# Token numbers and bias columns loaded as rows and turned by TensorE, all expert weights turned by SyncE's queue, and other orders around the expert tries

## The reference

```
x = x + attn(layernorm(x))      # linear attention, 16 heads of 32: q = k = x@Wqk + bqk, elu; v, u = silu(x@Wv + bv), silu(x@Wu + bu)
                                # kv = k^T v, out = q kv, out = layernorm(out, ln_g, ln_b); (u * out)@Wo + bo
x = x + experts(layernorm(x))   # token number picks one of 4 experts (numbers above 25000 are clipped):
                                # y = (silu(x@W[e].T) * (x@W[e].T))@W[e].T, the same ctx weights three times
x = x + ffn(layernorm(x))       # W_up, W_gate, W_down (512 x 2048), each rounded to -1, 0, 1 times its mean magnitude
```

## Time and profile before

| | |
|---|---|
| Time, median of 3 runs | 680.95 us (679.29 to 681.01) |
| The profiled execution, its own time | 680.71 us |
| its span in the profile | 678.9 us |
| TensorE busy with matmuls | 659.8 us, 97% |
| VectorE, ScalarE, GpSimd busy | 504.2, 294.8, 210.6 us |
| mean granted TensorE clock | 0.995 |

### The profile page before, as it was taken

The page is one execution under the profiler, slowest core; times in us unless marked ns, Lnnn a source line. Parts: engine busy times, 40 slices in busy tenths (PEclk is TensorE's granted clock), DMA queues, the critical chain, the costliest instruction groups (busy, mean ns, idle before and its releaser), DMA issues.

```text
span 678.9 us, 11797 instructions
## 1 busy us (share of the span) xinstructions
PE 659.8 (97%) x4435; PEld 430.0 (63%) x4465; DVE 504.2 (74%) x818; ACT 294.8 (43%) x435; POOL 210.6 (31%) x221
## 2 busy tenths in 40 slices
PE   8989999999999979999999999999999999999996
PEld 7446546546547565555556777777777777777772
DVE  6676683773754869998986986887878886676665
ACT  4475664555545254554332533342433433332331
POOL 4032543034025300001220535326343644324222
PEclk9989999999999999999999999999999999999999
DMA  7948069059058275973320111113030211101001
GB/s 197 376 150 239 1 177 258 0 126 276 31 124 261 97 269 161 252 205 94 71 55 2 30 27 28 28 28 90 1 55 2 56 62 28 28 1 63 1 1 62
DMA packets 91444, 68.15 MB, mean 100 GB/s; under 512 B 71681, under 2 KB 71681, under 8 KB 90369
## 3 DMA queue, kind: packets, MB, share of 16 engines
q1 hardware_dynamic: 88832, 59.03, 32.4%
q0 software_dynamic: 2560, 8.42, 3.4%
HBM read 42.51 MB, written 8.41 MB: 75 GB/s over the span
## 4 chain that ended last, share of the span: by engine, by line
PE 84%; DMA 7%; SPq 3%; DVE 2%; ACT 2%; issue 1%; POOL 0%; POOLq 0%; DVEq 0%; ACTq 0%
PE bank L1350 34%; PE bank L1637 28%; PE bank L1646 15%; DMA stage<-in_L_ffn_W_up_dram 4%; PE bank L1343 3%; PE bank L1516 1%; SPq L220 1%; PE bank L1538 1%; DMA late<-n 1%; PE bank L1502 1%; ACT stage L578 1%; DMA stage<-in_L_ffn_W_gate_dram 1%; DMA stage<-in_L_ffn_W_down_dram 1%; SPq L234 0%; DMA sorted_residual<-rows,pos 0%
## 5 line engine op out<-in xcount | busy, mean ns | idle before, releaser
L1637 PE MATMUL bank<-w_att,region 128*128 128x256 f16 x1024 | 127.6, 273 | 0.0
L1646 PE MATMUL bank<-region,w_moe 128*128 128x512 bf16 x482 | 113.8, 379 | 2.3 <-DVE w_moe L1260 0.8
L1637 PEld LDWEIGHTS bank<-w_att,region 128*128 128x128 bf16 x1024 | 100.1, 98 | 18.2 <-DVE tmpA L1275 0.2
L1350 PE MATMUL bank<-late,w_att 128*128 128x512 f16 x384 | 86.2, 383 | 0.3 <-DMA late<-n 0.3
L1271 DVE TENSOR_TENSOR n<-bank,n 128x512 f32<-128x512 f32 x112 | 71.4, 685 | 18.9 <-PE bank L1637 17.1
L491 POOL TENSOR_TENSOR w_moe<-tmp,w_moe 128x512 f16<-128x512 f32 x30 | 39.2, 1307 | 139.1 <-ACT w_moe L734 139.1
L1646 PEld LDWEIGHTS bank<-region,w_moe 128*128 128x128 f16 x512 | 50.0, 98 | 48.8 <-DVE w_moe L1260 1.3
L727 ACT ACTIVATE n<-n,qs 128x512 f32<-128x512 f32 x64 | 44.5, 719 | 64.6 <-DVE n L1271 64.6
L1637 PE MATMUL bank<-w_att,late 128*128 128x256 f16 x512 | 66.4, 273 | 0.0
L1350 PEld LDWEIGHTS bank<-late,w_att 128*128 128x128 f16 x384 | 37.8, 99 | 44.3 <-issue 1.8
L1637 PEld LDWEIGHTS bank<-w_att,late 128*128 128x128 bf16 x512 | 50.0, 98 | 12.1
(11 more groups left out here) (178 smaller groups left out, 1057.5 us busy)
## 6 DMA issues: line engine op xcount, KB each, us to landing
stage<-in_L_ffn_W_up_dram SPq DMA_DIRECT2D x8, 1024.0 KB, 7.2
stage<-in_L_ffn_W_gate_dram SPq DMA_DIRECT2D x8, 1024.0 KB, 6.8
rows<-sorted_residual SPq DMA_DIRECT2D x16, 257.5 KB, 3.0
stage<-in_ctx_dram SPq DMA_DIRECT2D x4, 1024.0 KB
stage<-in_L_ffn_W_down_dram SPq DMA_DIRECT2D x4, 1024.0 KB
nrm<-in_L_ffn_W_down_dram SPq DMA_DIRECT2D x4, 1024.0 KB, 7.7
rows<-in_x_dram SPq DMA_DIRECT2D x1, 3072.0 KB, 16.2
rows<-in_x_dram SPq DMA_DIRECT2D x4, 256.0 KB, 3.5
```

Source lines behind the costliest of these rows:

```text
L1350: mm = pe.matmul(dst, lhs(*step), rhs(*step), start=(start and n == 0), stop=(stop and n == len(steps) - 1))
L1637: mm = pe.matmul(wk_ps[bank][:, q * H:(q + 1) * H], w[:, c + q, k * P:(k + 1) * P], x3S_part[slot][:, h, m, k], start=(h == 0 and k == 0), ...
L1646: mm = pe.matmul(ffy_ps[t][:, :], hid[:, u, h, q, (t % 2) * P:(t % 2 + 1) * P], tern[2][:, c + q], start=(begins and q == 0 and h == 0), s ...
```

## The change

The token numbers and the four vectors are loaded as rows of 128 elements into free space of `region`, ahead of Wv. TensorE turns them into the bank `prep` between the queries' first and second parts, and VectorE copies them out to `cols` and `tokf`. Expert 0 goes the way of the others: one `ctx_half_hi`, one `ctx_half_lo`, two DMA turns. In batch 0 the load of expert 1's weights now stands ahead of `batch_turned(1)`, and ScalarE loads its Exp table before the third `magnitudes` instead of after. In the last batch the first part of `u_part(0)` stands ahead of the head products. Ahead of the tries the two first `keep_busy` have 14 and 66 matmuls instead of 52 and 16. Tiles 14 and 15 are turned by DMA as the tiles 3 to 13 are, so that their normalising and cutting fall a step or two earlier. In step 0 VectorE makes `negative(0)` after `h_mul(0)`, and `h_lo(0)` before `xs_lo(2)`; `hidden_lo` is the old `h_lo` with its wait. The diff, cut to its core:

```diff
 # SyncE: loads
-        def column_in(i, v):
-            sp.dma_start(cols[:, i], column(v), allow_slow_non_contiguous=True).then_inc(s["cols_in"], 16)
-
-        column_in(0, bqk)
+        for i, v in enumerate((bqk, bu, ln_g, ln_b)):
+            sp.dma_start(col_rows[K * i:K * i + K, :], v.rearrange("(k p) -> k p", p=P)).then_inc(s["cols_in"], 16)
+        sp.dma_start(tok[:, :], tok_v).then_inc(s["tok_in"], 16)
         sp.dma_start(att_slot[1], att_v[1]).then_inc(s["att_in1"], 16)
-        sp.dma_start(tok[:, :], tok_v, allow_slow_non_contiguous=True).then_inc(s["tok_in"], 16)
-        for i, v in ((1, bu), (2, ln_g), (3, ln_b)):
-            column_in(i, v)
...
         def weights(b):
 
-            if b > 0:
-                weights_turned(b, 0)
+            weights_turned(b, 0)
             sp.wait_ge(s["abs_done"], 3 * b + 1)
             summed_unit(b, 1)
-            if b > 0:
-                weights_turned(b, 1)
+            weights_turned(b, 1)
             sp.wait_ge(s["abs_done"], 3 * b + 2)
             summed_unit(b, 2)
-            if b > 0 and b + 1 < B:
+            if b + 1 < B:
                 expert_weights(b + 1)
-            if b + 1 < B:
                 batch_turned(b + 1)
-            if b == 0:
-                sp.wait_ge(s["ctx_mm"], 4)
-                expert_weights(1)
-            if b + 1 < B:
                 sp.wait_ge(s["abs_done"], 3 * b + 3)
                 summed_unit(b + 1, 0)
...
-        for i in range(3, NT - 2):
+        for i in range(3, NT):
             tile_turned(i)
...
 # ScalarE, batch 0
             if first:
-                ctx_hi(b, 0)
+                ctx_half_hi(b, last)
...
-                if first and m < 3:
-                    ctx_hi(b, m + 1)
...
+            act.wait_ge(s["exp_loaded"], b)
+            act.activation(spare[:, :], cols[:, 0, 0:1], ACT.Exp).then_inc(s["exp_loaded"], 1)
             if first:
                 magnitudes(b, 2)
-            act.wait_ge(s["exp_loaded"], b)
-            act.activation(spare[:, :], cols[:, 0, 0:1], ACT.Exp).then_inc(s["exp_loaded"], 1)
...
 # VectorE
+            dve.wait_ge(s["turned_rows"], 1)
+            dve.tensor_copy(cols[:].rearrange("p i k -> p (i k)"), prep[:, 0:4 * K]).then_inc(s["cols_made"], 1)
+            route(dve.tensor_copy(tokf[:, :], prep[:, 4 * K:4 * K + NT]))
...
                 routing_starts()
-                ctx_lo(b, 0)
                 routing_bases()
+                ctx_half_lo(b, last)
                 dve.wait_ge(s["x_rest"], 16)
...
                 first_stats(b + 1)
-                ctx_lo(b, 1)
                 split(3)
-                ctx_lo(b, 2)
                 first_norm(b + 1, True)
-                ctx_lo(b, 3)
...
 # VectorE, expert tries
-            if i == 0 or i + 1 in (NT - 2, NT - 1):
-                xs_lo(i + 1)
-            if i + 2 < NT - 2:
+            if i == 0:
+                xs_lo(1)
+                negative(0)
+                hidden_lo(0)
+            if i + 2 < NT:
                 xs_lo(i + 2)
-            if i + 2 in (NT - 2, NT - 1):
-                xs_norm(i + 2)
-            elif i + 3 < NT - 2:
+            if i + 3 < NT:
                 xs_norm(i + 3)
...
 # TensorE, batch 0 and the last batch
+                pe.wait_ge(s["cols_in"], 64)
+                pe.transpose(prep[:, 0:4 * K], col_rows[:, :], ident[0:4 * K, 0:4 * K])
+                pe.wait_ge(s["tok_float"], 1)
+                pe.transpose(prep[:, 4 * K:4 * K + NT], tok_rows[:, :], ident[0:NT, 0:NT]).then_inc(s["turned_rows"], 1)
                 pe.wait_ge(s["x_lo"], T)
...
             pe.wait_ge(s["w_lo"], 3)
-            if not last:
+            if last:
+                u_part(b, 0, first, [(0, 0)])
+            else:
                 for m in range(K):
                     u_part(b, m, first)
-                    if first and m < 3:
-                        ctx_part(b, m + 1)
...
-        u_part(B - 1, 0, False)
+        u_part(B - 1, 0, False, REST)
...
-        keep_busy(ps[0], 52)
+        keep_busy(ps[0], 14)
         unit_transposes(0, 0)
-        keep_busy(ps[0], 16)
+        keep_busy(ps[0], 66)
         unit_transposes(0, 1)
         keep_busy(ps[0], 16)
```

More of the change, by code:

```diff
@@ L190, in decoder @@
         ident_made pool_const started scatter_out starts_made bias_added rs1_first rs1 rs_o rs_o_last rs2 rs2_last rs3
-        w_hi_half w_hi w_lo ctx_mm ctx_hi ctx_lo ctx_half_hi ctx_half_lo ctx_in abs_done abs_mm scale_step
+        w_hi_half w_hi w_lo ctx_half_hi ctx_half_lo ctx_in abs_done abs_mm scale_step
         route_step route_pos steps_made route_mm route_read route_ready
@@ L250, in weights_turned @@
             if h:
-                sp.wait_ge(s["ctx_half_lo"], T * b)
+                sp.wait_ge(s["ctx_half_lo"], T * b + T)
             else:
-                sp.wait_ge(s["ctx_half_hi"], b)
+                sp.wait_ge(s["ctx_half_hi"], b + 1)
             sp.dma_start_transpose(out=w_moe[:, b, h].rearrange("p k (r s) -> p (k r) s", s=P),
@@ L542, in split @@
             act.activation(w_att[:, m, 0], att_slot[m], ACT.Copy).then_inc(s["w_hi"], 1)
-        def ctx_hi(b, k):
-            act.wait_ge(s["ctx_mm"], 4 * b + k + 1)
-            act.activation(w_moe[:, bass.ds(b, 1), 0, k].rearrange("p a d -> p (a d)"), prep[:, :], ACT.Copy,
-                           scale=CTX_SCALE).then_inc(s["ctx_hi"], 1)
         def ctx_half_hi(b, last):
@@ L663, in _ @@
         split(1)
-        act.wait_ge(s["cols_in"], 64)
+        act.wait_ge(s["cols_made"], 1)
         batch(0, True, False)
@@ L900, in _ @@
         first_lo(3)
+        dve.wait_ge(s["tok_in"], 16)
+        dve.tensor_copy(tok_rows[:, :], tok[:, :]).then_inc(s["tok_float"], 1)
         split(0)
         routing_members()
-        dve.wait_ge(s["cols_in"], 64)
+        dve.wait_ge(s["cols_made"], 1)
         def gated_mul(b, k, last=False):
@@ L959, in ctx_half_lo @@
         def ctx_half_lo(b, last):
-            dve.wait_ge(s["ctx_half_hi"], b)
+            dve.wait_ge(s["ctx_half_hi"], b + 1)
             hi, lo = (ctx_place(b, last, h).rearrange("p (k r s) -> p r k s", k=K, r=T) for h in range(2))
@@ L964, in ctx_half_lo @@
                                          op0=ALU.mult, op1=ALU.subtract).then_inc(s["ctx_half_lo"], 1)
-        def ctx_lo(b, k):
-            dve.wait_ge(s["ctx_hi"], 4 * b + k + 1)
-            hi = w_moe[:, bass.ds(b, 1), 0, k].rearrange("p a d -> p (a d)")
-            lo = w_moe[:, bass.ds(b, 1), 1, k].rearrange("p a d -> p (a d)")
-            dve.scalar_tensor_tensor(out=lo, in0=prep[:, :], scalar=CTX_SCALE, in1=hi, op0=ALU.mult,
-                                     op1=ALU.subtract).then_inc(s["ctx_lo"], 1)
         def q_elu(b, m, bank=None):
@@ L1196, in weight_sum, with hidden_lo @@
             dve.tensor_tensor(dst[j], a[j], b[j], op).then_inc(s[done], 1)
+        def hidden_lo(i):
+            dve.wait_ge(s["h_hi"], i + 1)
+            dve.tensor_tensor(hT[:, 1], th_ps[:, :], hT[:, 0], ALU.subtract).then_inc(s["h_lo"], 1)
         def expert_step(i):
@@ L1223, in expert_step @@
                 negative(i)
-            dve.wait_ge(s["h_hi"], i + 1)
-            dve.tensor_tensor(hT[:, 1], th_ps[:, :], hT[:, 0], ALU.subtract).then_inc(s["h_lo"], 1)
+            if i > 0:
+                hidden_lo(i)
             if i in (9, 10):
@@ L1239, in _ @@
         xs_norm(2)
-        negative(0)
         for i in range(STEPS):
@@ L1353, in _ @@
         ones_b = ones[:, :].bitcast(BF16)
+        REST = [(1, 0), (0, 1)]
         def keep_busy(bank, n):
@@ L1408, in project, with u_part @@
                 product(*operands(t)).then_inc(s["wo_mm"], 1)
-        def u_part(b, m, first):
+        def u_part(b, m, first, pairs=PARTS):
+            operands = (acc[m % 2][:, :], lambda i, j, k: w_att[:, 2, j, k, m * P:(m + 1) * P], lambda i, j, k: xT[:, i, k])
+            if pairs == REST:
+                partial(*operands, pairs, range(K), False, True).then_inc(s["u_mm"], 1)
+                return
             if m < 2:
@@ L1417, in u_part @@
                 pe.wait_ge(s["u_act"], K * b + m - 1)
-            product(acc[m % 2][:, :], lambda i, j, k: w_att[:, 2, j, k, m * P:(m + 1) * P],
-                    lambda i, j, k: xT[:, i, k]).then_inc(s["u_mm"], 1)
+            mm = partial(*operands, pairs, range(K), True, pairs == PARTS)
+            if pairs == PARTS:
+                mm.then_inc(s["u_mm"], 1)
         def batch(b, first, last):
@@ L1482, in batch @@
                 transposes(tr[t % 2], lambda k: qT[:, k, t * P:(t + 1) * P]).then_inc(s["tk_mm"], 1)
-            if first:
-                pe.wait_ge(s["stage_in0"], 16)
-                ctx_part(b, 0)
             pe.wait_ge(s["w_lo"], 3)
-            if not last:
+            if last:
+                u_part(b, 0, first, [(0, 0)])
+            else:
                 for m in range(K):
                     u_part(b, m, first)
-                    if first and m < 3:
-                        ctx_part(b, m + 1)
```

35 lines of the change are left out of this document (13 added, 22 removed).

## The result

The changed kernel is slower: 684.8 us (median of 8 runs, 683.4 to 686.1) against 680.45 us before (8 runs), ratio 1.0060, 95% interval 1.0048 to 1.0071. Forecast was 678.5. The profiled execution took 683.6 us with a span of 681.9, against 680.7 and 678.9.

What follows compares the result with a forecast made beforehand. TensorE, busy 97% of the span, was taken as the bound. Gains of 0.6 + 0.7 + 0.2 + 0.9 = 2.4 us took the profiled 680.7 to 678.3, 678.5 as a median; range 676.6 to 680.8.

Steps and rivals of the forecast that it cites:

- tiles 14 and 15: Late steps of the tries: turning these by DMA saves TensorE two turns of 0.44 us each, 0.9 us in all.
- The clock: Rival: granted clock falls in a new wait, costing 1.7 us once (680.2), both places 681.9; chance 0.2.
- the first of its two places: Batch 0, between `kv_mm` and `o_mm`: TensorE would stand still for 3 us, from 51 to 54.
- The second place: Ahead of the tries, behind 14 constant matmuls: a new TensorE wait of 2.5 us, from 234.6 to 237.1.
- The front: Batch 0's loads and ScalarE's chain up to batch 1's first query: gain 0.3 to 1.3 us, taken as 0.6.
- Last batch: Ahead of `kv_mm`: four matmuls of `u_part(0)` fill TensorE's 0.73 us wait for ScalarE's copies; gain 0.7 us.
- Entry and step 0: Passage into the tries: `h_mul(0)` right after silu gains 1.1 us, delay ahead loses 0.9; net gain 0.2.
- the 66 matmuls: Constant matmuls before the second turn of signs: 3.9 us instead of 0.95, turn 1.36 late, 0.48 covered; loss 0.9.

Runs made afterwards that it cites:

- with GpSimd after `weight_sum`: Changed kernel with GpSimd's `x3_lo(0)` made to wait until VectorE's `weight_sum` of step 12 is over; ratio 1.0048 to the kernel before.
- filling the wait: Changed kernel with 90 constant matmuls put on TensorE between `kv_mm` and `o_mm` of batch 0; ratio 1.0027 to the kernel before.
- The rows alone: Kernel before with only token numbers and bias columns loaded as rows and turned by TensorE; ratio 0.9992 to the kernel before.

## Why the prediction was wrong

**The step that failed: tiles 14 and 15.** I took 0.44 us twice off TensorE, "with TensorE back to back before and behind". That is true of the turn. It left out that the same edit gives VectorE another `xs_lo` ahead of step 12, turns the operand of `xs_lo` from a bank into SBUF, and makes `weight_sum` start behind GpSimd, which holds it for 4.46 us instead of 1.22 and TensorE with it, for 0.41 and 2.21 us. Forecast −0.9; measured +2.7 in the tail and +3.1 in the median. The row that warned stood in the trace of before, an `xs_norm` of 2.39 us beside GpSimd where others take 0.54, and I did not read it, since nothing waited for it.

The Trainium skill (SBUF — State Buffer, SBUF: two separate sides) says that VectorE and GpSimd share a pair of ports under an exclusive lock, and that whichever starts first holds it "for the whole instruction". It names VectorE's instructions in a two-port fast mode, and those with two SBUF inputs beside a GpSimd instruction that reads SBUF. Two traces here agree: `weight_sum` of 1.22 us took 4.46 behind GpSimd, `xs_lo(15)` 3.76 instead of 0.68 (with GpSimd after `weight_sum`), and GpSimd's instruction of 0.25 us took 2.12 behind `split(3)`.

**The clock.** The rival was named and priced at 1.7 us, with a chance of 0.2. In the first of its two places it came, and filling the wait won back 2.2, of which the trace shows 0.6 in batch 1. What I had wrong is the chance: I took the wait as 3 us from a chain through ScalarE only, and it was 5.66, because I did not count `ctx_half_lo`'s 2.50 us on VectorE ahead of the statistics, nor GpSimd held up by `split(3)`. The second place was no trial of it: the forecast wait of 2.5 us never came, for the reason given below, and the clock was 1.00 from 236 to 242 us.

**The front.** Forecast −0.6 for batch 1. W_up, W_gate and the third sum came as forecast within 1.1 us, but batch 1 started 0.8 us later. Even with the clock held it starts at 59.57 and then waits 0.63 us for the second half of its input, which lands at 62.0 (60.8 to 61.8 was forecast), and its `kv_mask` (107.9) comes no earlier than before (107.7 and, again, 107.2). Nothing is gained there with expert 0 by DMA. The rows alone do gain there, 1.6 to 2.1 us by their trace, though their median can't be told from before.

**Last batch.** Forecast −0.7, measured −0.86: from `kv_mask` of batch 3 to `abs_mm` 13.12 us became 12.26. Right.

**Entry and step 0.** Forecast −0.2. From `abs_mm` to `h_mul(11)` three traces with the old order take 102.3 to 102.9 us (mean 102.7), eleven with the new one 101.3 to 102.4 (mean 101.7). The gain is 1.0 in the mean, 1.1 in the profiled change. The three of the eleven with expert 0 turned by TensorE have a mean of 102.2, the eight with it turned by DMA 101.5, so the new order by itself gives about 0.5; what gives the rest is not shown. The term that was mis-sized is the 66 matmuls: I charged 0.9 us. I had left out that the change also puts VectorE's `two_signs(0, True)` ahead of the last residual. So the first turn of signs starts at 235.99 without a wait, the 66 matmuls start 2.5 us earlier against `abs_mm` than I had them, and the second turn waits 0.76 us behind them: VectorE's next signs, held up by GpSimd's last memset, are not there earlier.

**The sum**, in medians: 3.1 lost at the tiles and 2.2 that filling the wait wins back, less 1.2 gained by the rest, is 4.1, and the result is 4.1 by its ratio and 4.35 by its medians.

## What to carry to other kernels

When an edit adds an instruction to VectorE, or turns the only operand that it had in PSUM into SBUF, look for GpSimd's long instructions in the steps behind it: an order that only just works (0.38 us here) is turned over by less than a microsecond of delay. Look in the trace of before for instructions that are longer than their kind, even where nothing waits for them. A move of work off TensorE that leaves it standing still can lose again by the clock behind the wait what the move won; 90 constant matmuls of 0.059 us bought 2.2 us here.
